# Taking the row maximum off the scores on GpSimd: tensor_scalar in place of tensor_tensor

## The reference

```
q, k, v = layernorm(x) @ w_q.T + b_q, ctx @ w_k.T + b_k, ctx @ w_v.T + b_v
scores  = einsum("bthd,bshd->bhts", q * 0.25, k) + attn_bias        # 8 x 16 heads of 512 x 512
scores  = where(key_padding_mask, -3.4e38, scores)
attn    = softmax(scores, axis=-1)
x       = x + (attn @ v) @ w_out.T + b_out
h       = silu(fp4(ln(x)) @ fp4(w_gate).T) * (fp4(ln(x)) @ fp4(w_up).T)   # 704 wide
x       = x + fp4(h) @ fp4(w_down).T
```

## Time and profile before

| what | value |
|---|---|
| median of 3 runs | 926.07 us (926.05 to 926.24) |
| the profiled execution | 926.77 us, of which the span 924.8 us |
| granted TensorE clock, mean | 0.996 of full |
| TensorE busy | 881.1 us, 95% of the span |
| VectorE busy | 709.4 us, 77% |
| ScalarE busy | 618.6 us, 67% |
| GpSimd busy | 534.8 us, 58% |
| GpSimd in `less_max` (L618) | 322.3 us in 308 instructions |

### The profile page before, as it was taken

One profiled execution on the slowest core, in us unless ns is written; L12 is line 12 of the kernel. 1 busy time (PEld: TensorE's weight loads), 2 busy tenths in 40 slices (PEclk: granted clock), 3 DMA queues, 4 the chain that ended last, 5 costly groups with the idle time before them and its releaser, 6 DMA issues.

```text
span 924.8 us, 20212 instructions
## 1 busy us (share of the span) xinstructions
PE 881.1 (95%) x6772; PEld 705.2 (76%) x6772; DVE 709.4 (77%) x1867; ACT 618.6 (67%) x1119; POOL 534.8 (58%) x501
## 2 busy tenths in 40 slices
PE   6699999999999999999999999989889999999997
PEld 5677777787777777777777776767568888888886
DVE  5767777776767766766776679899479999989984
ACT  2577777776777776777777777787755555555542
POOL 4877966876786786777778557875212222222222
PEclk9899999999999999999999999999999999999999
DMA  6587425343443533435244253600000000000000
GB/s 191 168 217 204 134 46 145 93 106 93 93 127 76 123 107 80 123 90 134 60 115 118 58 134 85 167 31 1 2 1 12 18 18 23 17 17 17 18 18 29
DMA packets 50796, 76.50 MB, mean 83 GB/s; under 512 B 5264, under 2 KB 22032, under 8 KB 50704
## 3 DMA queue, kind: packets, MB, share of 16 engines
q1 hardware_dynamic: 50448, 75.06, 30.5%
q10 hardware_dynamic: 256, 0.26, 0.1%
HBM read 45.16 MB, written 29.36 MB: 81 GB/s over the span
## 4 chain that ended last, share of the span: by engine, by line
PE 81%; ACT 6%; issue 5%; DVE 3%; DMA 3%; SPq 2%; POOL 1%; ACTq 0%; DVEq 0%
PE psum L1232 26%; PE psum L1376 12%; PE psum L1330 11%; PE psum L1583 9%; PE psum L1568 4%; PE psum L1567 4%; PE psum L1566 4%; PE psum L1294 3%; PE psum L1254 2%; ACT att L776 2%; PE psum L1260 2%; ACT att L783 1%; PE psum L1271 1%; DVE att L1093 1%; SPq L400 1%
## 5 line engine op out<-in xcount | busy, mean ns | idle before, releaser
L1093 DVE CUSTOM_DVE_ANT_0 att<-psum,att 128x512 f32<-128x512 f32 x512 | 341.9, 687 | 143.9 <-PE psum L1330 142.1
L618 POOL TENSOR_TENSOR att<-att,neg_max 128x512 f32<-128x512 f32 x308 | 322.3, 1057 | 167.4 <-DVE neg_max L1093 165.0
L1232 PE MATMUL psum<-ident,att 128*128 128x128 f32 x2576 | 379.8, 275 | 23.7 <-ACT att L776 8.2
L1232 PEld LDWEIGHTS psum<-ident,att 128*128 128x128 f32 x2576 | 310.8, 141 | 91.1 <-ACT att L776 30.0
L776 ACT ACTIVATE att<-psum 128x512 f32<-128x512 f32 x512 | 298.5, 599 | 114.9 <-PE psum L1232 110.5
L1330 PE MATMUL psum<-stack 128*128 128x512 f32 x512 | 249.9, 489 | 10.4 <-DMA stack<-q_hl 7.0
L701 POOL TENSOR_TENSOR att<-att 128x704 f32<-128x704 f32 x32 | 61.8, 1931 | 162.8 <-DVE att L1210 162.8
L783 ACT ACTIVATE att<-att,neg_max 128x512 f32<-128x512 f32 x204 | 147.5, 723 | 11.1 <-DVE neg_max L1093 11.0
L1330 PEld LDWEIGHTS psum<-stack 128*128 128x128 f32 x512 | 97.5, 191 | 43.0 <-issue 32.1
L1376 PE MATMUL psum<-att 128*32 128x256 f32 x2048 | 123.8, 382 | 0.0
L1583 PE MATMUL psum<-att 128*128 128x256 f32 x384 | 91.7, 380 | 2.7 <-ACT att L903 2.7
(11 more groups left out here) (105 smaller groups left out, 1083.1 us busy)
## 6 DMA issues: line engine op xcount, KB each, us to landing
stack<-qk_planes SPq DMA_DIRECT2D x124, 192.0 KB, 4.0
qk_planes<-k_hl SPq DMA_DIRECT2D x48, 256.0 KB
qk_planes<-q_hl SPq DMA_DIRECT2D x48, 256.0 KB
att<-in_fside_1xSxS_dram SPq DMA_DIRECT2D x32, 256.0 KB, 3.0
att<-in_ctx_dram SPq DMA_DIRECT2D x8, 512.0 KB, 7.5
out_dram<-att SPq DMA_DIRECT2D x32, 128.0 KB, 1.7
x<-in_x_dram SPq DMA_DIRECT2D x1, 2560.0 KB, 13.2
x<-in_x_dram SPq DMA_DIRECT2D x3, 512.0 KB, 5.4
```

Source lines behind the costliest of these rows:

```text
L618: pool.tensor_tensor(prob[:, slot, :], prob[:, slot, :], neg_max[:, slot:slot + 1].to_broadcast([P, S]), ALU.subtract).then_inc(less_pool, 1)
L1093: dve.tensor_tensor_reduce(out=prob[:, slot, :], in0=ps_score[:, SCORE_BANK[2 * S_ + r], :], in1=bias_m[:, tt, :], scale=-1.0, scalar=BIG, ...
L1232: return pe.transpose(out_, in_, ident[:, :])
```

## The change

The subtraction in GpSimd's `less_max` is issued as another instruction. Before, it was a `tensor_tensor` with two tensor inputs, the second being the 128 x 1 column `neg_max` read 512 times over by a broadcast access pattern. After, it is a `tensor_scalar` with one tensor input, and the column is given as the scalar of each partition; its second operation is left empty. Shapes, type (float32), the place of the result, the wait and the semaphore stay, and so do the order of the queue and the share of tiles that GpSimd has. ScalarE's `less_max` is not touched.

```
                 slot = (TILES * n + 2 * s + r) % RING
                 pool.wait_ge(biased, TILES * n + 2 * s + r + 1)
-                pool.tensor_tensor(prob[:, slot, :], prob[:, slot, :], neg_max[:, slot:slot + 1].to_broadcast([P, S]),
-                                   ALU.subtract).then_inc(less_pool, 1)
+                pool.tensor_scalar(prob[:, slot, :], prob[:, slot, :], neg_max[:, slot:slot + 1], None, ALU.subtract).then_inc(less_pool, 1)
```

## The result

| | before | after |
|---|---|---|
| median | 926.08 us (926.05 to 926.24, 4 runs) | 932.75 us (931.23 to 933.59, 4 runs) |
| ratio | | 1.0071, 95% interval [1.0059, 1.0083] |
| profiled execution, its span | 926.77, 924.8 us | 931.23, 929.2 us |

The change makes the kernel 0.7% slower, about 6.6 us. The forecast was no measurable change, 925.4 us with a range up to 930.0.

What follows compares the result with a forecast made beforehand. TensorE, with 81% of the chain that ended last, was taken as the bound. Profiled 926.77 us less 0.7 for shorter VectorE stalls gave 926.07; the median lying 0.7 lower, the forecast was 925.4 us, range 923.3 to 930.0.

Steps and rivals of the forecast that it cites:

- the price of the instruction: GpSimd's new 512-element subtraction was put at 0.90 us, between bounds of 0.52 and 2.4, against 1.04 before.
- rival 2: GpSimd becomes the bound, transposes waiting for its subtractions above 1.58 us each: slower, up to 1179 us; 18%.
- the prediction's own sum: Profiled 926.77 us less 0.7 us, from 5 x (1.04 - 0.90) at places on the chain, giving 926.07.
- The rest of the edit costs nothing: Wait, increment and queue order stay; low_q and low_k behind the subtractions may start up to 0.14 us sooner.
- The five places: Four VectorE stalls and one subtraction on the chain, 530 to 600 us, each ending earlier by the subtraction's shortening; 0.7 us.
- The edge at 1.58 us: GpSimd keeps up from 130 to 530 us while a subtraction takes under 1.58 us; beyond, each adds its excess.
- the even part: Attention from 130 to 530 us, TensorE busy 394.67 of 400 us and GpSimd 289.58; TensorE's time should stay within 1 us.
- The milder form of rival 2: With a subtraction of 1.41 to 1.58 us, the five places alone lose over 1.85 us: 928 to 929 us.
- no transpose waited for a subtraction: In attention each subtraction's result lies about 7.5 us before TensorE's transposes ask for it, so they never wait for it.
- VectorE stands for as long as GpSimd's instruction runs: VectorE's casts and two-input instructions begin only when GpSimd's current instruction ends, so its duration sets their stall.
- the time alone: VectorE's L1048 was said to take 0.75 us alone, against 1.25 us beside GpSimd's subtraction.

Runs made afterwards that it cites:

- fill168: The kernel before, tensor_tensor kept, with three memsets of 128 x 150 on spare memory behind each GpSimd subtraction; ratio 1.066.
- ts_middle: The kernel before with the change made in octets 2 to 12 alone, 220 of the 308 subtractions; ratio 0.9998.
- ts_relief_late: The changed kernel, with ScalarE also taking the maximum off all tiles with r = 1 in octets 11 and 12; ratio 1.0073.
- ts_scale_first: The changed kernel, with GpSimd's weights' scale queued ahead of its step's subtraction and the last batch's two bias instructions one step later; 1.0039, 929.19 us.
- ts_apply_late: The changed kernel, with VectorE's layernorm_apply for batch 2 and GpSimd's add_bo behind it moved three steps later in the first batch; ratio 1.0086.
- tt_scale_first: The kernel before, tensor_tensor kept, with the queue order of ts_scale_first; ratio 0.9991, 924.31 us.

## Why the prediction was wrong

**The failed step is the price of the instruction.** I took 0.90 us from bounds of 0.52 and 2.4; it is 1.57. The direction was wrong with it: 1.04 is the price of what went. Within the price it is the slope that failed. I gave the 480 further elements 0.83 to 1.65 ns each, from instructions of other kinds, and "one tensor is read in place of two" as the reason for the lower half; 0.90 us stands for 1.2 ns. The measured slope is 2.55, more even than the 2.3 ns of the AFFINE_SELECT, which I had used against rival 2. To take L626's 325 ns for 32 elements as mostly fixed was sound, since the fixed part is about 0.27 us (1575 - 512 x 2.55 ns), but a row of 32 elements says nearly nothing of a slope, and no row of before had one for this kind. The tight loop of the Trainium skill, GPSIMD Engine Reference, section 3.1, with 1.8 cycles an element and 768 ns for 512, was no guide to this instruction either: the measured slope is 3.1 cycles at its 1.2 GHz.

**A second step failed with it: the rest of GpSimd's queue was put at nothing.** With 1.57 us in it, the prediction's own sum gives 926.1 + 5 x 0.53 = 928.8 us, and 932.75 was measured. "The rest of the edit costs nothing" looked at `low_q` and `low_k` and at no other instruction that VectorE waits for. Those were the loss: rstd (L573), bias (L602) and scale (L625), 3.5 us before tile 80 and 2.9 us after tile 416. The five places that the sum did charge gave no loss: the VectorE instructions that stand beside a subtraction became shorter (last section).

**The edge at 1.58 us held and was beside the point.** The runs put it between the change and fill168. In the even part the new instruction just fits, and it costs nothing, as ts_middle shows. But the sum was made over the even part only. From 28 to 130 us, the first batch and the start of the second, gives 102 us with 80.32 busy, and 55 subtractions lie there (the trace of before): (102 - 80.32)/55 = 0.39 us of room each, an edge at 1.44. That was there to be read. Near 590 us the room is not short on average, but the order of the queue makes the scale wait behind long subtractions.

**The milder form of rival 2** (1.41 to 1.58 us, 928 to 929) came nearest. It had the price and the side, with 5 of rival 2's 18 points, but neither the place nor the size: it charged 5 x 0.5 us for VectorE's stalls beside the subtractions.

**What held.** In the changed kernel no transpose waited for a subtraction; in three variants (ts_relief_late, ts_scale_first, ts_apply_late) one did, for 0.3 to 0.6 us. The even part did not move. And the forecast that VectorE stands for as long as GpSimd's instruction runs was wrong in a way that helped the change, below.

## What to carry to other kernels

An engine that is off the critical path has as much room as its fullest stretch, not its mean, and what sits in its queue for other engines pays first: list every semaphore that the queue raises, and ask of each how late it may come. The share of an engine on the chain that ended last does not say what its slowness costs (42% here at no loss). A broadcast tensor_tensor with one column was a third cheaper on GpSimd than the tensor_scalar made for it, so an instruction's price is to be measured on its own kind and at two widths, not by how many tensors it reads. Where a hand-over is late, see first whether its queue is full (here only less work helped) or just badly ordered.

## What the runs showed of the hardware

**GpSimd's tensor_scalar lets VectorE in early.** Before, VectorE's casts and two-input instructions stood until near the end of GpSimd's tensor_tensor. I expected the longer instruction to hold them longer. They got shorter at the median, and VectorE's busy time fell from 709.4 to 703.2 us (answering to the earlier trace rows):

```profile
L971 DVE CAST k_hl<-att x16: 363/423/1416, 15.0 to 581.6; 128x512 fp32r<-128x512 f32 x16
...
L1047 DVE TENSOR_TENSOR att<-att,w_r x9: 692/897/1266, 546.8 to 635.5; 128x512 f32<-128x512 f32 x9
...
L1053 DVE SCALAR_TENSOR_TENSOR att<-att x9: 680/682/796, 551.9 to 640.1; 128x512 f32<-128x512 f32 x9
```

The median of the cast is 423 ns, where it was 815. Two overlaps show how:

```profile
37.92 1.56 POOL L618 TENSOR_SCALAR att<-att,neg_max 128x512 f32<-128x512 f32 x1
...
38.28 0.60 DVE L966 CAST q_hl<-att 128x512 fp32r<-128x512 f32 x1 [2.33 <-DMA qk_planes<-q_hl]
...
174.08 1.79 POOL L618 TENSOR_SCALAR att<-att,neg_max 128x512 f32<-128x512 f32 x1
...
174.98 0.42 DVE L966 CAST q_hl<-att 128x512 fp32r<-128x512 f32 x1
```

A cast that began 0.36 us into the instruction took 0.60 us in place of 0.42, so it stood until about 0.54 us in. One that began 0.90 us in ran at full speed, and the tensor_scalar took 1.79 us in place of 1.57. L1047, started at 592.09 and 0.33 us into the L618 of 591.76, took 0.90 us in place of 0.69, which again is a hold of about 0.54 us. (The 0.69 us is the shortest that this instruction took, 692 ns, also in tt_scale_first with the old subtraction; the 0.75 us that the prediction called the time alone was itself a little held.) Counted in the same way, every one of the 31 overlaps of these instructions in the trace of before ends its hold 0.90 us into the 1.04 us.

The rest of the overlaps after fit, but for two. All 23 that began 0.57 to 0.96 us into the tensor_scalar ran at full speed. What they did to it differs by kind: beside a cast begun 0.8 us in or later it took 1.69 to 1.84 us, beside the two-input L1047 1.57 or 1.58. Two casts that began 1.27 and 1.30 us in took 0.59 and 0.54 us.

The Trainium skill, SBUF — State Buffer, section Who interferes with whom, has the loser fully blocked for the whole instruction. For tensor_tensor the trace agrees roughly, with a hold to 0.90 of 1.04 us; for this tensor_scalar, with a hold to 0.54 of 1.57 us, it does not, and the measurement decides. Why the hold ends there is not settled by these runs.
